# Reordering the steps of four engines in a fused two-layer gated network

## The reference, cut to what matters

```python
    x = x + jnp.tanh(g_xattn[0]) * _L0_xattn_ref(_layernorm(x), ctx, ...)   # 1
    x = x + jnp.tanh(g_ffn[0]) * _L0_ffn_ref(_layernorm(x), ...)            # 2
    x = x + jnp.tanh(g_xattn[1]) * _L1_xattn_ref(_layernorm(x), ctx, ...)   # 3
    x = x + jnp.tanh(g_ffn[1]) * _L1_ffn_ref(_layernorm(x), ...)            # 4
    return x
```

## Time and profile before

| | |
|---|---|
| median of 3 runs | 374.71 us (371.63 to 375.29) |
| the profiled execution | 373.9 us, its span 372.1 us |
| TensorE busy | 300.9 us, 1518 matmuls |
| VectorE busy | 273.7 us |
| ScalarE busy | 217.8 us, 27 table loads in it |
| GpSimd busy | 112.3 us |
| chain that ended last | TensorE 60%, VectorE 31%, ScalarE 4% |
| transfers | 9.04 MB, nearly all in the first 28 us |

### The profile page before, as it was taken

One profiled execution on the slowest core, in us unless ns is written; L12 is line 12 of the kernel. 1 busy time (PEld: TensorE's weight loads), 2 busy tenths in 40 slices (PEclk: granted clock), 3 DMA queues, 4 the chain that ended last, 5 costly groups with the idle time before them and its releaser, 6 DMA issues.

```text
span 372.1 us, 5311 instructions
## 1 busy us (share of the span) xinstructions
PE 300.9 (81%) x1518; PEld 152.2 (41%) x1518; DVE 273.7 (74%) x1214; ACT 217.8 (59%) x453; POOL 112.3 (30%) x174
## 2 busy tenths in 40 slices
...
PEclk9995555689966589999999999999999999999989
...
DMA packets 2624, 9.04 MB, mean 24 GB/s; under 512 B 547, under 2 KB 548, under 8 KB 2340
## 3 DMA queue, kind: packets, MB, share of 16 engines
...
HBM read 7.66 MB, written 1.05 MB: 23 GB/s over the span
## 4 chain that ended last, share of the span: by engine, by line
PE 60%; DVE 31%; ACT 4%; issue 3%; DMA 1%; DVEq 0%
PE bank L457 59%; DVE R L1121 8%; DVE V L1114 6%; DVE MT L1024 5%; DVE arena L1024 4%; ACT arena L776 1%; DVE negm L1028 1%; DVE sel L1054 1%; DVE sm L1058 1%; DMA pack_kgen<-in_kgen 1%; DVE XG L1024 1%; DVE arena L1029 1%; DVE arena L1032 1%; ACT L773 1%; PE bank L538 1%
## 5 line engine op out<-in xcount | busy, mean ns | idle before, releaser
L776 ACT ACTIVATE arena<-bank 128x512 f32<-128x512 f32 (+3 forms) x75 | 38.5, 570 | 34.3 <-PE bank L457 23.2
L773 ACT ACT_TABLE_LOAD x27 | 34.6, 1283 | 28.6 <-PE bank L457 18.7
L457 PE MATMUL bank<-arena 128*32 128x16 f32 (+3 forms) x304 | 12.6, 226 | 41.6 <-DVE arena L1024 41.6
L1121 DVE MATCH_REPLACE8 R<-V,R 128x77 f32<-128x77 f32 x192 | 40.5, 221 | 0.0
L1087 DVE TENSOR_REDUCE pack_bfly<-bank 128x4 f32<-128x308 f32 x64 | 26.1, 468 | 8.9 <-PE bank L457 8.9
L1114 DVE MAX8 V<-R 128x8 f32<-128x77 f32 x192 | 31.2, 223 | 0.0
L457 PE MATMUL bank<-LO,pack_first 128*128 128x512 f32 x48 | 28.1, 678 | 3.1 <-ACT LO L776 2.8
L457 PE MATMUL bank<-arena,pack_dft 128*128 128x256 f32 (+1 forms) x96 | 29.5, 458 | 0.9 <-ACT arena L776 0.7
L457 PEld LDWEIGHTS bank<-arena 128*32 128x32 f32 (+1 forms) x304 | 10.4, 154 | 45.4 <-DVE arena L1024 42.0
L776 ACT ACTIVATE RS<-bank,cst 128x512 f32<-128x512 f32 x24 | 16.5, 688 | 20.3 <-PE bank L457 19.8
L1388 POOL TENSOR_TENSOR k0bd<-sel,w 128x308 f32<-128x308 f32 x16 | 13.3, 828 | 40.2 <-DVE w L1028 39.9
...
## 6 DMA issues: line engine op xcount, KB each, us to landing
...
```

Source lines behind the costliest of these rows:

```text
L457: return nc.tensor.matmul(out, lhsT, rhs, start=start, stop=stop, **kw)
L773: nc.scalar.add_instruction(mybir.InstLoadActFuncSet(name=nc.get_next_instruction_name(), act_func_set_id=need, ins=[], outs=[]))
L776: return nc.scalar.activation(out, in_, func, **kw)
L1121: nc.vector.match_replace(R8[:, g % 2, r % 2, h, :], V8[:, g % 2, h, r, :], src, NEG)\
```

## The change

All four lists of ORDER are rearranged; every word stays, so each engine has the same instructions on the same data. The waits and the banks are worked out anew from the lists. The first half of the lists changes most; of the rest the diff below shows two lines of ScalarE's.

```diff
 ORDER = {
     "pe": """
-        center0/0 s_k0 var0/0 weigh0/0 s_pc0 s_m0 score0/0 center0/1 score1/0 weigh1/0 var0/1 s_vw score2/0 vw/0
-        s_w1 weigh2/0 score3/0 s_kern0 s_trig weigh3/0 s_ufly attnT/0 s_kern1 s_kern2 s_kern3 film_in/0 s_pexp
-        s_psin0 score0/1 weigh0/1 s_freq xt/0 score1/1 weigh1/1 dft/0 s_parg0 s_t1 s_qsin center0/2 s_wup mix/0
-        s_qarg weigh2/1 s_qexp score2/1 vw/1 weigh3/1 film_pre/0 top2/0 idft/0 score3/1 center1/0 var0/2 vw/2
-        center0/3 s_bup s_plag score0/2 film_out/0 var1/0 attnT/1 film_in/1 film_pre/1 xt/1 score1/2 dft/1 ffn_up0/0
-        ffn_up1/0 ffn_down/0 weigh0/2 score2/2 var2/0 vw/3 idft/1 s_t2 score3/2 center2/0 film_out/1 center1/1
-        weigh1/2 center3/0 s_qlag s_wdn x1/0 var3/0 s_dfly weigh2/2 top2/1 k1/0 var1/1 s_consts weigh3/2 var0/3
-        s_dhigh fold_up0/0 ffn_up0/1 ffn_up1/1 attnT/2 score0/3 fold_up1/0 fold_down/0 film_in/2 score1/3 s_masks
-        ffn_down/1 center4/0 mix/1 xt/2 var2/1 s_qc var4/0 dft/2 k1/1 s_dlow q/0 weigh0/3 film_pre/2 scoreA0/0
-        s_psin1 center3/1 top2/2 var3/1 score2/3 idft/2 s_psin2 fold_up0/1 fold_up1/1 s_cols fold_down/1 weigh1/3
...
+        s_k0 s_qsin center0/0 var0/0 s_pexp s_m0 s_trig center0/1 weigh2/1 score0/0 score1/0 s_vw score2/0 s_w1
+        var0/1 s_plag score3/0 attnT/0 vw/0 s_kern0 s_kern1 film_in/0 score0/1 center0/2 s_kern2 weigh3/1 s_kern3
+        score1/1 s_freq xt/0 dft/0 score2/1 s_t1 film_pre/0 score3/1 idft/0 s_wup var0/2 top2/0 center0/3 s_pc3 x1/2
+        s_bup vw/1 weigh1/2 s_psin2 center1/0 score0/2 var1/0 weigh1/1 film_out/0 attnT/1 film_in/1 film_pre/1
+        score1/2 xt/1 mix/0 dft/1 s_parg0 s_coef s_t2 ffn_up0/0 ffn_up1/0 score2/2 x1/0 s_qexp mix/2 s_masks
+        ffn_down/0 s_wdn s_qlag weigh3/0 weigh3/3 s_pc0 mix/1 var2/0 idft/1 k1/0 film_out/1 s_misc score3/2
+        center1/1 s_dlow vw/2 center3/0 var3/0 s_pc1 var1/1 vw/3 var0/3 fold_up0/0 ffn_up0/1 ffn_up1/1 score0/3
+        fold_up1/0 attnT/2 fold_down/0 film_in/2 score1/3 center4/0 ffn_down/1 weigh2/2 xt/2 var4/0 var2/1 dft/2
+        center3/1 q/0 scoreA0/0 var3/1 k1/1 weigh0/2 score2/3 film_pre/2 fold_up0/1 fold_up1/1 idft/2 s_ufly
+        film_out/2 s_consts s_psin1 center2/0 fold_down/1 s_psin0 scoreA1/0 center1/2 center4/1 s_cols weigh2/0
...
     """,
     "act": """
-        s_kgen0 s_qlag center0/0 var0/0 s_m0 center0/1 s_vw score0/0 var0/1 s_trig score1/0 s_plag score2/0 s_qexp
-        s_qsin s_psin0 s_psin1 s_cols score3/0 vw/0 s_pexp s_psin2 s_psin3 s_kern1 attnT/0 s_kern3 score0/1 s_freq
-        xt/0 dft/0 s_t1 s_wup score1/1 vw/1 film_pre/0 center0/2 score2/1 score3/1 var0/2 center1/0 vw/2 var1/0
-        score0/2 attnT/1 xt/1 film_pre/1 dft/1 score1/2 ffn_up0/0 ffn_up1/0 center2/0 vw/3 var2/0 score2/2 s_t2
-        center3/0 center1/1 score3/2 center0/3 s_wdn k1/0 var3/0 var1/1 var0/3 fold_up0/0 ffn_up0/1 ffn_up1/1
-        fold_up1/0 attnT/2 score0/3 center2/1 center4/0 xt/2 var2/1 var4/0 score1/3 dft/2 q/0 film_pre/2 k1/1
-        center3/1 var3/1 fold_up0/1 fold_up1/1 score2/3 center1/2 center4/1 var1/2 var4/1 ffn_up0/2 ffn_up1/2 maxT/0
...
-        var3/2 film_pre/3 k1/3 var5/0 fold_up0/2 center1/3 fold_up1/2 units0/0 logits/0 units1/0 maxT/1 var1/3
-        keyA0/1 ffn_up0/3 ffn_up1/3 top2/0 keyA1/1 center4/2 center2/3 keyA2/1 var2/3 normA/1 center3/3 var4/2
...
+        s_kgen0 s_qlag center0/0 var0/0 s_m0 s_pexp score0/0 s_trig center0/1 score1/0 s_plag s_vw score2/0 var0/1
+        s_qsin s_qexp score3/0 s_psin0 s_psin1 attnT/0 vw/0 s_kern1 s_psin2 s_psin3 s_cols s_kern3 score0/1 s_freq
+        xt/0 score1/1 dft/0 score2/1 center0/2 s_t1 film_pre/0 score3/1 var0/2 s_wup center1/0 center0/3 vw/1 var1/0
+        attnT/1 score0/2 xt/1 film_pre/1 score1/2 dft/1 ffn_up0/0 s_t2 ffn_up1/0 center2/0 s_wdn var2/0 score2/2
+        k1/0 center1/1 vw/2 center3/0 score3/2 var3/0 vw/3 var1/1 var0/3 fold_up0/0 ffn_up0/1 ffn_up1/1 fold_up1/0
+        score0/3 attnT/2 center4/0 score1/3 center2/1 xt/2 var4/0 var2/1 dft/2 center3/1 q/0 var3/1 k1/1 score2/3
+        film_pre/2 fold_up0/1 fold_up1/1 center1/2 var1/2 center4/1 var4/1 ffn_up0/2 ffn_up1/2 score3/3 maxT/0
...
+        var5/0 film_pre/3 fold_up0/2 fold_up1/2 center1/3 logits/0 units0/0 maxT/1 var1/3 keyA0/1 ffn_up0/3
+        ffn_up1/3 units1/0 keyA1/1 center2/3 keyA2/1 center4/2 top2/0 var2/3 normA/1 center3/3 var4/2 var3/3 k1/3
...
     """,
     "dve": """
-        s_consts s_kgen0 s_masks s_k0 s_qarg var0/0 s_coef score0/0 score1/0 score2/0 s_w1 s_parg0 var0/1 score3/0
-        s_parg1 weigh3/0 s_qc s_pc0 s_pc1 s_pc2 s_pc3 s_cols s_kern1 s_kern3 film_in/0 score0/1 score1/1 mix/0
-        score2/1 film_pre/0 film_out/0 score3/1 var0/2 weigh3/1 s_bup score0/2 film_in/1 film_pre/1 var1/0 score1/2
-        mix/1 score2/2 var2/0 film_out/1 x1/0 score3/2 var3/0 var1/1 weigh3/2 var0/3 score0/3 film_in/2 fold_down/0
-        score1/3 var2/1 var4/0 x1/1 mix/2 film_pre/2 scoreA0/0 var3/1 score2/3 film_out/2 fold_down/1 scoreA1/0
...
+        s_kgen0 s_k0 s_masks s_consts s_qarg var0/0 s_coef score0/0 score1/0 score2/0 s_w1 s_parg0 var0/1 score3/0
+        weigh3/0 s_qc s_pc0 s_pc1 s_parg1 s_pc2 s_pc3 s_cols s_kern1 s_kern3 film_in/0 score0/1 score1/1 mix/0
+        score2/1 film_pre/0 film_out/0 score3/1 var0/2 weigh3/1 s_bup score0/2 film_in/1 var1/0 film_pre/1 score1/2
+        mix/1 score2/2 var2/0 film_out/1 x1/0 score3/2 var3/0 var1/1 var0/3 weigh3/2 score0/3 fold_down/0 film_in/2
+        score1/3 var4/0 var2/1 x1/1 mix/2 scoreA0/0 var3/1 score2/3 film_pre/2 film_out/2 s_misc fold_down/1
...
     """,
     "pool": """
         s_ufly s_coef weigh0/0 weigh1/0 s_qal weigh2/0 weigh3/0 var0/0 var0/1 s_udense mix/0 weigh0/1 s_dfly
-        weigh1/1 weigh2/1 weigh3/1 var0/2 s_dhigh mix/1 s_dlow weigh0/2 weigh1/2 weigh2/2 s_v1 k1/0 weigh3/2 mix/2
-        var0/3 weigh0/3 weigh1/3 weigh2/3 weigh3/3 k1/1 mix/3 k1/2 k1/3
+        weigh1/1 weigh2/1 weigh3/1 s_dhigh s_dlow mix/1 weigh0/2 var0/2 weigh1/2 weigh2/2 weigh3/2 k1/0 k1/1 mix/2
+        weigh0/3 s_v1 weigh1/3 weigh2/3 weigh3/3 var0/3 mix/3 k1/2 k1/3
     """,
 }
```

More of the change, by code:

```diff
@@ L105 @@
-        weigh2/3 scoreA1/0 center1/2 s_pc1 center4/1 scoreA2/0 var1/2 film_out/2 s_v1 scoreA3/0 mix/2 var4/1
-        ffn_up0/2 ffn_up1/2 s_pc2 score3/3 maxT/0 s_coef keyA0/0 ffn_down/2 keyA1/0 mixA0/0 keyA2/0 x1/1 mixA1/0
-        attnT/3 var2/2 normA/0 film_in/3 mixA2/0 xt/3 dft/3 wo/0 s_pc3 k1/2 s_parg1 center3/2 center5/0 center2/1
-        x1/2 k1/3 q/1 var3/2 film_pre/3 var5/0 scoreA0/1 idft/3 s_kgen0 film_out/3 scoreA1/1 fold_up0/2 center1/3
-        scoreA2/1 fold_up1/2 scoreA3/1 units0/0 logits/0 units1/0 maxT/1 var1/3 keyA0/1 fold_down/2 ffn_up0/3 s_misc
@@ L110 @@
-        center4/2 ffn_up1/3 keyA1/1 ffn_down/3 keyA2/1 var2/3 s_qal mixA0/1 normA/1 mixA1/1 mixA2/1 center3/3 var4/2
-        expand/0 var3/3 wo/1 q/2 center5/1 fold_up0/3 scoreA0/2 fold_up1/3 center2/2 var5/1 scoreA1/2 fold_down/3
-        scoreA2/2 spread0/0 spread1/0 center4/3 x1/3 scoreA3/2 logits/1 var4/3 center2/3 units0/1 moe_out/0 q/3
-        maxT/2 units1/1 expand/1 scoreA0/3 keyA0/2 spread0/1 spread1/1 scoreA1/3 scoreA2/3 keyA1/2 top2/3 scoreA3/3
-        mixA0/2 keyA2/2 weigh3/3 maxT/3 mixA1/2 keyA0/3 mixA2/2 keyA1/3 normA/2 mixA0/3 wo/2 keyA2/3 center5/2
@@ new lines @@
+        center3/1 q/0 scoreA0/0 var3/1 k1/1 weigh0/2 score2/3 film_pre/2 fold_up0/1 fold_up1/1 idft/2 s_ufly
+        film_out/2 s_consts s_psin1 center2/0 fold_down/1 s_psin0 scoreA1/0 center1/2 center4/1 s_cols weigh2/0
+        scoreA2/0 var1/2 s_v1 scoreA3/0 var4/1 score3/3 ffn_up0/2 weigh1/0 ffn_up1/2 maxT/0 ffn_down/2 s_kgen0
+        keyA0/0 keyA1/0 weigh0/1 mixA0/0 mixA1/0 attnT/3 keyA2/0 film_in/3 var2/2 normA/0 xt/3 top2/2 mixA2/0 s_qarg
+        dft/3 wo/0 center3/2 x1/1 weigh0/3 q/1 k1/2 center5/0 normA/3 weigh1/3 top2/1 var3/2 film_pre/3 var5/0
@@ new lines @@
+        scoreA0/1 idft/3 scoreA1/1 fold_up0/2 film_out/3 scoreA2/1 fold_up1/2 center1/3 scoreA3/1 logits/0 units0/0
+        var1/3 maxT/1 s_pc2 keyA0/1 fold_down/2 ffn_up0/3 ffn_up1/3 s_qal units1/0 keyA1/1 ffn_down/3 weigh0/0
+        keyA2/1 center4/2 var2/3 mixA0/1 s_dhigh mixA1/1 normA/1 mixA2/1 s_udense center3/3 var4/2 k1/3 var3/3 wo/1
+        center2/1 expand/0 q/2 center5/1 fold_up0/3 scoreA0/2 fold_up1/3 scoreA1/2 var5/1 fold_down/3 scoreA2/2
+        spread0/0 weigh3/2 center2/3 spread1/0 center4/3 logits/1 var4/3 scoreA3/2 moe_out/0 units0/1 s_parg1 q/3
```

27 lines of the change are left out of this document (14 added, 13 removed).

## The result

| | before | after |
|---|---|---|
| median, beside each other | 374.06 us (371.63 to 375.29, 5 runs) | 379.39 us (374.96 to 379.45, 5 runs) |
| the profiled execution | 373.9 us, span 372.1 us | 374.96 us, span 373.2 us |

What follows compares the result with a forecast made beforehand. Filter generation, then VectorE and TensorE in turns were taken to bound it up to 162.2 us, TensorE afterwards. +4.4 - 5.3 - 1.0 = -1.9 us gave 372.8 us from a median of 374.71; range 368.0 to 380.0.

Steps and rivals of the forecast that it cites:

- What bounds the kernel: Up to 162.2 us filter generation, then VectorE and TensorE in turns; afterwards TensorE, so fold_up0/0's shift moves the end.
- Term 1: First 67 us, filter generation: VectorE stalls for s_psin2, score0/1 starts at 83.2 us against 78.8, +4.4 us.
- The short end, +2: Low bound of the first 67 us' cost: GpSimd's step at 1.7 us and TensorE at full clock.
- Term 2: From score0/1 to fold_up0/0: VectorE's waits shrink from 7.2 to 1.8 us, film_in/1 at full clock, -5.3 us.
- Term 3: Behind 162.2 us: fewer TensorE waits around idft/2 and at xt/3, -1.0 us.
- the frame: Whatever fold_up0/0's start shifts by, the end shifts by, unless TensorE gets new stops behind 162.2 us.
- The sum: Whole kernel: +4.4 - 5.3 - 1.0 = -1.9 us, faster, 372.8 us on the median.
- A: Clock stays at half behind s_bup, film_in/1 and film_pre/1 take 7.2 us: 377.3 us, up to 380; chance 0.24.
- B: Kernel generation does not stall, or TensorE keeps its clock from 100 us on: 369 us; chance 0.22.
- C: Waits only trade places, VectorE's and TensorE's work untouched: no change, 374.7 us; chance 0.16.

Runs made afterwards that it cites:

- qexp_back: Changed kernel with one ScalarE word moved back, s_qexp ahead of s_qsin: 377.99 us, ratio 1.0115 to the kernel before.
- short kind: Executions of the changed kernel between 374.6 and 375.6 us, 10 of 23; the profile that came with the result is one.
- long kind: Executions of the changed kernel between 378.1 and 379.5 us, 13 of 23; profiled later, film_in/1 and film_pre/1 took 6.08 us.
- aft_same_chip: The changed kernel itself, unedited, timed again beside the kernel before: 378.23 us, ratio 1.0105; its profiled execution is a long one.
- gen_old_tail: Changed kernel with the lists of before up to the second search and from fold_up0/0 on: 374.24 us, ratio 0.9894 to the kernel before.
- gen_old_same_chip: Changed kernel with all four lists of before up to the second search, beside the changed kernel on one chip: 371.81 us, ratio 0.9956 to the kernel before.

## Why the prediction was wrong

- **What bounds the kernel** held: of the 6.85 us at film_in/0 6.8 reached the end.
- **Term 1** (+4.4 forecast, +6.2 measured at score0/1). The stall, its place and its size (3.2 against 3.69 us) were right. Two steps of the sum were mis-sized. "s_qsin starts only 0.4 us later than now": it started at 41.72 us, 1.5 earlier than before, and with it s_qal. "VectorE ends score3/0 at about 56.1 us": 58.2, since two instructions met s_qal and not one. qexp_back shows that mending this gives nothing as long as the chain over GpSimd ends last. The short end, +2, was not to be had, as said there.
- **Term 2** (-5.3 forecast, -5.6 in the short kind, -2.2 to -2.4 in the long). In the short kind the number is right to 0.3 us, by two offsets: less waiting for TensorE (0.3 us for 1.8), but 0.6 us of waiting for ScalarE and 0.6 us more work of VectorE's own (76.3 us busy for 75.7). The step that failed is "So I take film_in/1 and film_pre/1 at full clock": going by the times, it holds in 10 of 23 executions. I argued from 5.8 us of work behind which the clock had come back once. It did come back in the long kind too, at 125.5 us; what I had not reckoned with is that it falls again 3.25 us later, under film_in/1. This step costs 3.6 to 4.3 us (376.8 and 377.5 us of span against 373.2) and makes the median.
- **Term 3** (-1.0 forecast, +0.4 measured). -1.3 us up to 295 us; the same distances, 132.0 and 133.3 us, stand in aft_same_chip and in gen_old_tail, which has the lists of before there. It was given back by a stretch at half clock from 322 us, which I had not looked for: the frame took TensorE's work as the same sum behind 162 us, and its clock was not.
- **The sum.** Short kind +6.2 - 5.6 + 0.4 = +1.0 us, the spans say +1.1. Long kind some 4 more. Even in the short kind the sign was wrong, by 1.8 us of term 1 and 1.4 of term 3.
- **The rivals.** A has the place of what the longer executions do (film_in/1 at half clock) and nearly the time (fold_up0/0 at 165.8 forecast, 166.41 and 167.11 measured). Its mechanism is not theirs, and its time was partly luck, as said above. A loss at this place had 0.24 and should have had about half. B is excluded by the stall and the half clock at idft/0, C by the filter stage's 6.85 us, of which the middle gave back only a part.

What decides between the kinds stays open. The stretch at half clock behind s_bup is 3.25 us in one and 6.5 in the other, and in the long kind the next fall comes 3.25 us of full clock later, under film_in/1; why the stretch differs is not shown. The kinds part before it. In the changed kernel's own traces idft/0's stretch at half clock is 6.5 us in the short kind (103.75 to 110.25 us) and 3.25 in the long (105.25 to 108.5 and 106.25 to 109.25), and the clock, at half from about 26 us on, is back at 76.5 us in the short and at 71.25 and 72.0 in the long. gen_old_same_chip has 6.5 us at idft/0 and film_in/1 at half clock nonetheless, so that this alone does not decide it either. Whether s_bup's place is to blame was not settled either, since both kernels that moved it in the new order made something else wait.
